# Folding mirrored rows on GpSimd, a ring of exp(k) rows, and the order of VectorE's taps in a two-block image kernel

## The chip, the cores and the metric

The kernel runs on one core of a Trainium2 chip, as one launch. The metric is device microseconds from the first to the last work of that launch, the median of several runs. One execution was also taken by the hardware profiler; all rows below are of that one.

## The reference

Eight images of 96 channels and 96 x 96 pixels go through two residual blocks, each behind a group norm of three channels a group (`x = x + L0(gn(x))`, `x = x + L1(gn(x))`), all in float32.

L0 makes four depthwise seven-tap filters of the image (along a row, a column and both diagonals), takes the mean of the squares of each, sends these 4 x 96 numbers through two small dense layers and a softmax over the four directions, adds up the four filtered images with these weights, and convolves the sum 3 x 3 with 96 x 96 channels.

L1 is attention over channels. It uses the image in two ways:

- `k = softmax(Wk x)` and `v = Wv x`, whose product over all pixels is a 24 x 24 context for each of four heads; `q = softmax(Wq x)`, times the context, times a projection, is `out`.
- `qf = real(ifft2(W_q2 gelu(W_q1 real(fft2(x)))))` and the keys from `out` give, normalized, a second channel attention, whose values are a 3 x 3 depthwise convolution of a projection of `out`.

The kernel before folds all small matrices of L1 into one 3 x 3 convolution of exp(q) per image. What needs the pixels is: the maxima of k and q, the two-dimensional Fourier transform of W_q1 x (with GELU behind it), exp(k) times v, the transform of exp(k), and Gram products of the two transforms.

## The kernel before, in words

Each of the five engines runs its own program: image 0's L0, then a loop in which the attention block (L1) of image b-1 runs beside the taps of L0 of image b, then the last L0, and the last L1 alone. Seven attention blocks so have another image's taps beside them, and the eighth has none. Engines wait for one another only by semaphores, in the order written. That order is by hand; no planner chooses it.

Within one attention block TensorE goes through a list of uses of five PSUM slots (`stage`, lines 901 to 910), and another engine empties each slot before its next use:

- 36 uses for the maxima of k and q (lines 950 to 957), which VectorE reduces (lines 708 to 712);
- 24 uses of four image rows each, W_q1 times x, written by ScalarE to `z` with the row index last (lines 526 to 530, 991 to 997);
- a first transform of 36 uses (`dft`, lines 959 to 974): for each 8 channels two uses of the first stage (four channels each, one product of 96 columns a channel against `w_dft`, cosines and sines side by side) and one use of the second stage (two products, with `dcos` and `dnsin`); ScalarE writes the first stage to `s1` and the second, through GELU, to `t_sp` (lines 532 to 540);
- 48 uses of two neighbouring rows each for k and v; ScalarE writes exp(k) to `z` and v to a ring of four (lines 542 to 546); three uses later TensorE adds v times exp(k) to the context (`ctx_rows`, lines 976 to 981), with exp(k) read from `z`, where neighbouring channels lie 96 elements apart;
- a second transform of 36 uses, of exp(k), and 49 Gram products (lines 1018 to 1024);
- 24 uses for exp(q), the e tiles (lines 983 to 987 and 548 to 556), mixed with a chain of small products for the attention weights.

Beside this VectorE and ScalarE make the next image's four filtered images in twelve units (`unit`, line 93): a unit is two directions of 16 rows. ScalarE makes the first tap of each direction and later squares the result (`unit_work`, lines 502 to 511); VectorE makes the other six taps of each, twelve instructions a unit (`taps`, lines 687 to 706). ScalarE puts its unit work between evictions, one piece every four uses, a new unit every `UNIT_USES` = 20 uses (lines 513 to 520). VectorE makes units 2 to 8 behind the maxima and only then begins the chain for the attention weights (`attention_weights`, line 728), which first waits for the Gram products; units 9 to 11 come behind it:

```
for u in range(2, LEAD):
    taps(b, u)
...
edge_rows(b, NCH - 1)
taps(b, LEAD, 0, LEAD_TAPS)
...
attention_weights(i, chain)
```

with `LEAD` = 8 and `LEAD_TAPS` = 12. ScalarE has its work for units 7 and 8 between the second transform and the e tiles (lines 608 to 612).

GpSimd clears padding, makes a few powers of single columns and issues the DMAs of the residual and the output; in the attention block its first instruction waits for the Gram products (line 399). SyncE issues the other DMAs, which the change leaves as they are.

Of the kernel before, what the change touches and what calls it, by code (L numbers as in the profile page):

```python
# [21 lines left out]
F32 = mybir.dt.float32  # L22
# [6 lines left out]
N = H * W  # L29
# [32 lines left out]

DFT_ORDER = []
for _j in range(C // 8 + 1):
    if _j < C // 8:
        DFT_ORDER += [(1, 2 * _j), (1, 2 * _j + 1)]
    if _j >= 1:
        DFT_ORDER.append((2, _j - 1))
assert len(DFT_ORDER) == U_DFT


# [55 lines left out]
def build(nc, a, out):  # L127
    with ExitStack() as ctx:
# [3 lines left out]
        def sem(name):  # L132
# [10 lines left out]
        z = nc.alloc_sbuf_tensor_at("z", [W, C, H], F32, offset=lo0)  # L143
        t_sp = nc.alloc_sbuf_tensor_at("t_sp", [H, NV, 2 * C], F32, offset=lo0 + H * C * 4)
        assert (H * C + NV * 2 * C) * 4 <= 2 * EBYTES
        SBYTES = CR * W * 4
        arena2 = sb("arena2", [128, SBYTES // 4])
        s0 = nc.sbuf_base - SBYTES

        s1 = nc.alloc_sbuf_tensor_at("s1", [H, 2, 8, W], F32, offset=s0)  # L150
        a32 = nc.alloc_sbuf_tensor_at("a32", [C, 9, C], F32, offset=s0)
# [6 lines left out]
        vrow = sb("vrow", [W, VROWS, 2, C])  # L158
        etile = sb("etile", [C, ETILES, TR * W])
        wp_hi, wp_lo = sb("wp_hi", [C, 9, C], F32R), sb("wp_lo", [C, 9, C], F32R)  # L160
        a_hi, a_lo = sb("a_hi", [C, 9, C], F32R), sb("a_lo", [C, 9, C], F32R)
        bk = sb("bk", [C, 9, C])
        wkv = sb("wkv", [C + 1, 2 * C])
        mats = sb("mats", [C, 12, C])
        ident, group, mask, negmask, w_dft, dcos, dnsin, wq, wq1, wq2, wq2t, wpft = (
            mats[:, i, :] for i in range(12))
        wc = sb("wc", [C, C])
# [61 lines left out]
        max_part = sem("max_part")  # L229
        stage_evac = sem("stage_evac")  # L230
        l1_small, l1_ps = sem("l1_small"), sem("l1_ps")
        maxrow_ready, gram_done, l1_pow, l1_exp = map(sem, ("maxrow_ready", "gram_done", "l1_pow", "l1_exp"))
# [16 lines left out]
        def rows(buf, r0, n, dx=0):  # L249

            at = (r0 + 1) * EP + 1 + dx
            return buf[:, at:at + n * EP].rearrange("p (r c) -> p r c", c=EP)[:, :, 0:W]

        def small_chain(eng, s, total, i):
# [54 lines left out]
        def _(sp):  # L309
            loads = [(mats[:, n, :], a[k]) for n, k in enumerate(  # L310
                ("ident", "group", "mask", "negmask", "w_dft", "dcos", "dnsin", "wq", "wq1", "wq2", "wq2t", "wpft"))]
            loads += [(wkv[0:C, :], a["wkv"]), (wh[:], a["wh"]), (wv[:], a["wv"]), (w45[:], a["w45"]),
# [66 lines left out]
        def _(pool):  # L379
# [5 lines left out]
            def zero_pads():  # L385
                for e in (e_hi, e_lo):
# [61 lines left out]
        def _(act):  # L448
# [83 lines left out]
            def dft(i, at, ch0, func):  # L532
                for n, (kind, g) in enumerate(DFT_ORDER):
                    ps = stage(i, at + n)
                    if kind == 1:
                        act.activation(s1[:, (g // 2) % 2, (g % 2) * 4:(g % 2) * 4 + 4, :],
                                       ps[0:H, 0:4 * W].rearrange("p (c v) -> p c v", v=W), ACT.Identity).then_inc(stage_evac, 1)
# [104 lines left out]
        def _(dve):  # L642
# [202 lines left out]
            def step(b, first, second, more):  # L845
# [9 lines left out]
                if first:  # L855
                    for u in range(2, LEAD):
                        taps(b, u)

                    dve.wait_ge(tap_done, unit_taps(b, LEAD - 1, KT - 1, 0 if first_image(b) else 1))
                    if first_image(b):  # L860
                        dve.wait_ge(last_dir_sums, LEAD)
# [32 lines left out]
        def _(pe):  # L894
# [64 lines left out]
            def dft(i, at):  # L959
                for n, (kind, g) in enumerate(DFT_ORDER):  # L960
                    ps = stage(i, at + n)
                    if kind == 1:
                        if g == 0:
                            evacuated(i, at - 1)
                        for c in range(4):
                            last = pe.matmul(ps[0:H, c * W:(c + 1) * W], z[:, 4 * g + c, :], w_dft, start=(c == 0), stop=(c == 3),  # L966
                                             skip_group_check=True)
                    else:
                        first_of = [k for k, v in enumerate(DFT_ORDER) if v == (1, 2 * g + 1)][0]
                        evacuated(i, at + first_of)  # L970
                        d = ps[0:H, 0:8 * NV].rearrange("p (c v) -> p c v", v=NV)
                        pe.matmul(d, dcos, s1[:, g % 2, :, 0:NV], start=True, stop=False)  # L972
                        last = pe.matmul(d[:, :, 1:NV - 1], dnsin, s1[:, g % 2, :, NV:W], start=False, stop=True)  # L973
                    last.then_inc(stage_full, 1)

            def ctx_rows(i, g):
                evacuated(i, AT_KV + g)
                for r in range(2):
                    last = pe.matmul(ctx_ps[0:C, 0:C], vrow[:, g % VROWS, r, :], z[:, :, 2 * g + r],  # L979
                                     start=(g == 0 and r == 0), stop=(g == U_KV - 1 and r == 1))  # L980
                return last
# [7 lines left out]
            def attention_block(i, between):  # L989
                maxes(i)  # L990
                for g in range(U_ROWS):
                    ps = stage(i, AT_ROWS + g)
                    for r in range(TR):
                        h = g * TR + r
                        last = pe.matmul(ps[0:W, r * C:(r + 1) * C], x1[0:C, h * W:(h + 1) * W], wq1,  # L995
                                         start=(r == 0), stop=(r == TR - 1), skip_group_check=True)
# [7 lines left out]
                for g in range(U_KV + BEHIND):  # L1004
                    if g < U_KV:
                        ps = stage(i, AT_KV + g)
                        for r in range(2):
                            h = 2 * g + r
                            last = pe.matmul(ps[0:W, r * 2 * C:(r + 1) * 2 * C], x1[:, h * W:(h + 1) * W], wkv[:],  # L1009
# [106 lines left out]

NAMES = ["x", "ident", "group", "mask", "negmask", "w_dft", "dcos", "dnsin", "wq", "wq1", "wq2", "wq2t", "wpft",
         "wkv", "wh", "wv", "w45", "w135", "wk3", "temp", "att1", "att2", "wp", "w_mid", "wkvv"]

# [49 lines left out]
```

## Time and profile before

| | before |
|---|---|
| median of 3 runs | 3964.45 us (3962.36 to 3966.53) |
| profiled execution | 3964.9 us, span 3963.1 us |
| TensorE busy | 3760.3 us, 95% |
| TensorE weight loads busy | 3091.5 us, 78% |
| VectorE busy | 3030.4 us, 76% |
| ScalarE busy | 1624.7 us, 41% |
| GpSimd busy | 210.3 us, 5% |
| granted TensorE clock, mean | 0.982 of 2.4 GHz |

Busy shares are means over the whole span: an engine at 76% can be at 100% in one stage and idle in another. In a timeline or a group of instructions a row gives start, duration, engine, line and shape; the bracket at the end is the idle time of the engine just before, and what ended it. Matmuls overlap, so their cost is read from start to start and not from the duration. A float32 product appears as two records. PE is TensorE's matmuls, PEld its weight loads, DVE VectorE, ACT ScalarE, POOL GpSimd.

### The profile page before, as it was taken

To read this page: it belongs to the slowest core of one execution; us is meant where nothing else is said; L and a number is where in the kernel's file an instruction comes from. 1 tells how busy PE (TensorE), PEld (TensorE's weight loads), DVE (VectorE), ACT (ScalarE), POOL (GpSimd) and SP (SyncE) were. 2 spreads that over 40 slices of the span, in tenths; PEclk is the share of its full clock that TensorE was granted. 3 is DMA by queue.
4 is the path that set the end of the run, shared out by engine and by line. 5 is a ranking of instruction groups with operands and counts; after the bars stand their busy time and mean duration, and the time that the engine had idled before them with its cause. 6 is when DMAs were issued, how large, how long until landed. Compare 5 with 4: busy or idle time off the path is not lost.

```text
span 3963.1 us, 56863 instructions
## 1 busy us (share of the span) xinstructions
PE 3760.3 (95%) x21394; PEld 3091.5 (78%) x21394; DVE 3030.4 (76%) x2829; ACT 1624.7 (41%) x2912; POOL 210.3 (5%) x376
## 2 busy tenths in 40 slices
PE   4659999999999999999999999999999999999998
PEld 2348788978799687977889787996879777897977
DVE  7988988789778898679887897789986797753020
ACT  3413662237521564126622375215641266202430
POOL 1001000100001000000001000010001000010000
PEclk8879999999999999999999999999999999999999
DMA  4354222923156221732228231562217322260002
GB/s 112 97 147 112 65 64 44 218 63 77 37 124 168 59 65 39 178 98 65 64 47 214 63 77 40 122 166 60 68 36 194 82 74 55 53 163 25 1 7 30
DMA packets 164717, 344.13 MB, mean 87 GB/s; under 512 B 110336, under 2 KB 110576, under 8 KB 164432
## 3 DMA queue, kind: packets, MB, share of 16 engines
q1 hardware_dynamic: 141392, 255.36, 26.1%
q0 software_dynamic: 23040, 84.95, 9.8%
q8 instruction: 181, 2.97, 0.3%
q14 instruction: 104, 0.85, 0.1%
HBM read 189.27 MB, written 150.99 MB: 86 GB/s over the span
## 4 chain that ended last, share of the span: by engine, by line
PE 77%; DVE 12%; issue 7%; ACT 2%; DMA 1%; POOL 0%; SPq 0%; DVEq 0%; ACTq 0%; POOLq 0%
PE banks L941 15%; PE banks L942 15%; PE banks L947 15%; DVE feat L702 7%; PE banks L979 6%; PE banks L956 6%; PE banks L1009 6%; PE banks L966 4%; PE banks L1021 3%; PE banks L972 2%; PE banks L973 2%; DVE e_lo L725 2%; DMA feat<-feats_d 1%; DVE e_hi L718 1%; PE banks L995 0%
## 5 line engine op out<-in xcount | busy, mean ns | idle before, releaser
L702 DVE SCALAR_TENSOR_TENSOR feat<-xin,w,feat 96x1536 f32<-96x1536 f32 x540 | 943.2, 1808 | 1.1
L941 PE MATMUL banks<-e_hi,wp_hi 96*96 96x384 f32 x1728 | 587.6, 341 | 23.4 <-DVE e_lo L828 12.0
L941 PE MATMUL banks<-e_hi,a_hi 96*96 96x384 f32 x1728 | 591.9, 343 | 15.2 <-ACT a_hi L572 15.2
L942 PE MATMUL banks<-e_lo,a_hi 96*96 96x384 f32 x1728 | 590.1, 342 | 0.0
L942 PE MATMUL banks<-e_lo,wp_hi 96*96 96x384 f32 x1728 | 586.6, 340 | 0.0
L702 DVE SCALAR_TENSOR_TENSOR feat<-xin,wh,feat 96x1536 f32<-96x1536 f32 x288 | 520.5, 1807 | 43.8 <-ACT feat L488 42.9
L702 DVE SCALAR_TENSOR_TENSOR feat<-xin,wv,feat 96x1536 f32<-96x1536 f32 x288 | 520.5, 1807 | 8.9 <-ACT feat L488 8.9
L500 ACT ACTIVATE sqjunk<-feat 96x1536 bf16<-96x1536 f32 x192 | 284.4, 1481 | 258.7 <-DVE feat L702 255.8
L563 ACT ACTIVATE res<-banks 96x768 f32<-96x768 f32 x96 | 77.5, 808 | 689.2 <-PE banks L947 689.2
L947 PE MATMUL banks<-e_hi,a_lo 96*96 96x384 f32 (+1 forms) x1728 | 337.1, 339 | 0.0
L947 PE MATMUL banks<-e_hi,wp_lo 96*96 96x384 f32 (+1 forms) x1728 | 336.1, 338 | 0.0
L966 PEld LDWEIGHTS banks<-mats,z 96*96 96x96 f32 x3072 | 288.0, 165 | 57.7 <-issue 46.8
L941 PEld LDWEIGHTS banks<-e_hi,wp_hi 96*96 96x96 f32 x1728 | 281.3, 163 | 51.4 <-DVE e_lo L828 12.4
L941 PEld LDWEIGHTS banks<-e_hi,a_hi 96*96 96x96 f32 x1728 | 283.3, 164 | 48.6 <-issue 16.1
L979 PE MATMUL banks<-z,vrow 96*96 96x96 f32 x1536 | 312.9, 339 | 3.5 <-ACT vrow L546 3.5
L1009 PE MATMUL banks<-wkv,x 97*96 97x192 f32 x1536 | 315.5, 328 | 0.0
L942 PEld LDWEIGHTS banks<-e_lo,a_hi 96*96 96x96 f32 x1728 | 283.8, 164 | 27.7
L942 PEld LDWEIGHTS banks<-e_lo,wp_hi 96*96 96x96 f32 x1728 | 281.6, 163 | 27.6
L947 PEld LDWEIGHTS banks<-e_hi,a_lo 96*96 96x96 f32 x1728 | 279.6, 163 | 26.4
L947 PEld LDWEIGHTS banks<-e_hi,wp_lo 96*96 96x96 f32 x1728 | 278.6, 162 | 26.1
L966 PE MATMUL banks<-mats,z 96*96 96x96 f32 x3072 | 289.9, 248 | 2.6 <-ACT z L529 2.6
L1009 PEld LDWEIGHTS banks<-wkv,x 97*96 97x96 f32 x1536 | 255.8, 170 | 7.1 <-issue 6.3
(147 smaller groups left out, 4921.7 us busy)
## 6 DMA issues: line engine op xcount, KB each, us to landing
feats_d<-feat SPq DMA_DIRECT2D x160, 576.0 KB, 4.1
feat<-feats_d SPq DMA_DIRECT2D x160, 576.0 KB, 6.5
feat<-in_x SPq DMA_DIRECT2D x48, 576.0 KB, 7.1
res<-in_x POOLq DMA_DIRECT2D x96, 288.0 KB, 4.1
out<-x POOLq DMA_DIRECT2D x96, 288.0 KB, 2.8
out<-res POOLq DMA_DIRECT2D x96, 288.0 KB, 4.4
xin<-in_x SPq DMA_DIRECT2D x32, 792.0 KB, 8.9
xin<-in_x SPq DMA_DIRECT2D x16, 684.0 KB, 9.9
```

The source lines that it names most:

```text
L500: act.activation(sqjunk[:], feat[:, d], ACT.Square, accum_out=sq[:, d, ch:ch + 1]).then_inc(squared, 1)
L702: dve.scalar_tensor_tensor(out=dst, in0=src, scalar=taps_w[d](k), in1=dst, op0=ALU.mult, op1=ALU.add).then_inc(tap_done, 1)
L725: dve.tensor_tensor(rows(e_lo, t * TR, TR), etile[:, t % ETILES].rearrange("p (r c) -> p r c", c=W), rows(e_hi, t * TR, TR).bitcast(F32), ...
L941: pe.matmul(dst, whi[:, t, :], rows(e_hi, a0, n, dx), start=(t == CENTRE_FIRST[0]), stop=False)
L942: pe.matmul(dst, whi[:, t, :], rows(e_lo, a0, n, dx), start=False, stop=False)
L947: last = pe.matmul(dst, wlo[:, t, :], rows(e_hi, a0, n, dx), start=False, stop=(t == CENTRE_LAST[-1]))
L956: pe.matmul(ps[0:C, :], w, x1[0:C, t * BANK:(t + 1) * BANK], start=True, stop=True)\
L966: last = pe.matmul(ps[0:H, c * W:(c + 1) * W], z[:, 4 * g + c, :], w_dft, start=(c == 0), stop=(c == 3), skip_group_check=True)
L972: pe.matmul(d, dcos, s1[:, g % 2, :, 0:NV], start=True, stop=False)
L979: last = pe.matmul(ctx_ps[0:C, 0:C], vrow[:, g % VROWS, r, :], z[:, :, 2 * g + r], start=(g == 0 and r == 0), stop=(g == U_KV - 1 and r == 1))
L1009: last = pe.matmul(ps[0:W, r * 2 * C:(r + 1) * 2 * C], x1[:, h * W:(h + 1) * W], wkv[:], start=(r == 0), stop=(r == 1), skip_group_check=True)
L1021: pe.matmul(gram_ps[0:C, 2 * C:4 * C], t_sp[:, v, 0:C], t_sp[:, v, :], start=(v == 1), stop=(v == NV - 2))
```

## The change

Rows h and 96-h enter a Fourier transform along h with the same cosine and opposite sines. The change adds and subtracts such rows before the transform, in both uses.

- GpSimd writes `xf`, the sums (49 rows) and differences (47 rows) of normalized image rows, in `fold_x`; W_q1 is applied to those. It waits chunk by chunk for the normalized image, and TensorE waits for all of it before its 24 uses.
- The k,v uses take rows g and 96-g instead of two neighbours. ScalarE writes exp(k) not to `z` but to a ring of six row pairs (`krow`, in the memory of the e tiles). The context product reads that ring. GpSimd reads it too, and writes sums and differences to `z` (`fold_k`: 49 instructions an image). ScalarE waits for `k_folded` before it writes over a pair, and TensorE waits for all folds before the second transform.
- The transform has 24 uses instead of 36. A use of the first stage takes 8 channels, each with two products of 49 columns: 49 summed rows (in a block of 64) with cosines to partitions 0 to 63, 47 differences with sines to partitions 64 to 110. The second stage is one product over those 111 partitions with `dh`. The order is 8 first, 4 second, 4 first, 8 second. `s1` has eight slots, in two pieces of memory.
- `UNIT_USES` is 18. VectorE's loop is rewritten around `last_use` = 7; `LEAD_TAPS` is gone.

The diff, cut:

```
-U_DFT = C // 4 + C // 8
+U_DFT = 2 * (C // 8)
...
+DFT_ORDER = ([(1, g) for g in range(8)] + [(2, g) for g in range(4)]
+             + [(1, g) for g in range(8, 12)] + [(2, g) for g in range(4, 12)])
+KROWS = 6
+X_FOLDS = [(41, 7)] + [(h, 8) for h in range(33, 0, -8)]
...
-LEAD_TAPS = TAPS // 2
-UNIT_USES, UNIT_AT = 20, AT_ROWS + 8
+UNIT_USES, UNIT_AT = 18, AT_ROWS + 8
...
+            def fold_x(i):
+                v = x1[0:C, :].rearrange("p (h x) -> p h x", x=W)
+                for h, n in X_FOLDS:
+                    up, down = v[:, h:h + n, :], v[:, H - h:H - h - n:-1, :]
+                    pool.wait_ge(xn_ready, i * XN + -(-(H - h + 1) * W // (N // XN)))
+                    pool.tensor_tensor(xf[:, h:h + n, :], up, down, ALU.add).then_inc(x_folded, 1)
+                    pool.tensor_tensor(xf[:, NV - 1 + h:NV - 1 + h + n, :], up, down, ALU.subtract).then_inc(x_folded, 1)
+                pool.tensor_copy(xf[:, 0:NV:NV - 1, :], v[:, 0:NV:NV - 1, :]).then_inc(x_folded, 1)
+            def fold_k(i):
...
+                def fold(g, n):
+                    s = g % KROWS
+                    one_, other = krow[:, s:s + n, 0, :], krow[:, s:s + n, 1, :]
+                    pool.tensor_tensor(z[:, :, g:g + n].rearrange("p c h -> p h c"), one_, other, ALU.add)\
+                        .then_inc(k_folded, 1)
+                    at = NV - 1 + g
+                    pool.tensor_tensor(z[:, :, at:at + n].rearrange("p c h -> p h c"), one_, other, ALU.subtract)\
+                        .then_inc(k_folded, 1)
+                row_evicted(1)
+                fold(1, 1)
+                pool.tensor_copy(z[:, :, 0:NV:NV - 1].rearrange("p c h -> p h c"), krow[:, 0, :, :]).then_inc(k_folded, 1)
+                for g in range(2, U_KV, 2):
+                    row_evicted(g + 1)
+                    fold(g, 2)
...
+                    fold_x(i)
+                    fold_k(i)
                     pool.wait_ge(gram_done, i + 1)
...
-                    act.activation(z[:, :, 2 * g:2 * g + 2], ps[:, :, 0:C].rearrange("p r c -> p c r"), ACT.Exp)
+                    if g >= KROWS:
+                        act.wait_ge(k_folded, i * K_FOLD_OPS + k_folds((g - KROWS) // 2 + 1))
+                    act.activation(krow[:, g % KROWS], ps[:, :, 0:C], ACT.Exp)
...
-                    for u in range(2, LEAD):
+                    last_use = UNITS - 5
+                    for u in range(2, last_use + 1):
                         taps(b, u)
...
-                    taps(b, LEAD, 0, LEAD_TAPS)
+                    for u in range(last_use + 1, LEAD + 1):
+                        taps(b, u)
                 if second:
                     attention_weights(i, chain)
                 if first:
-                    taps(b, LEAD, LEAD_TAPS)
...
-                        for c in range(4):
-                            last = pe.matmul(ps[0:H, c * W:(c + 1) * W], z[:, 4 * g + c, :], w_dft, start=(c == 0), stop=(c == 3),
-                                             skip_group_check=True)
+                        for c in range(8):
+                            cols = slice(c * NV, (c + 1) * NV)
+                            pe.matmul(ps[0:ODD_AT, cols], z[:, 8 * g + c, 0:ODD_AT], w_cos[:, 0:NV], start=(c == 0),
+                                      stop=(c == 7), skip_group_check=True)
+                            last = pe.matmul(ps[ODD_AT:FOLDED, cols], z[:, 8 * g + c, NV:W], w_sin[:, 0:NV],
+                                             start=(c == 0), stop=(c == 7), skip_group_check=True)
...
-                        pe.matmul(d, dcos, s1[:, g % 2, :, 0:NV], start=True, stop=False)
-                        last = pe.matmul(d[:, :, 1:NV - 1], dnsin, s1[:, g % 2, :, NV:W], start=False, stop=True)
+                        last = pe.matmul(ps[0:H, 0:8 * NV], dh[:], s1(g).rearrange("p c v -> p (c v)"), start=True, stop=True)
...
+                pe.wait_ge(x_folded, (i + 1) * X_FOLD_OPS)
...
+                pe.wait_ge(k_folded, (i + 1) * K_FOLD_OPS)
                 dft(i, AT_DFT2)
```

## Rows read from the trace of the kernel before

**Rows 1.** The page, part 4, the chain of waits, by engine.
```profile
PE 77%; DVE 12%; issue 7%; ACT 2%; DMA 1%; POOL 0%; SPq 0%; DVEq 0%; ACTq 0%; POOLq 0%
```

**Rows 2.** Busy time by stretch of one steady image; columns in the first line.
```profile
core 0: us, PE busy (x) PEld busy (x) DVE busy (x) ACT busy (x) POOL busy (x), PEclk, DMA share, GB/s
845.40:876.40 31.00, 30.97 (x72) 11.82 (x73) 28.80 (x39) 11.00 (x16) 0.00 (x0) 1.00 0.17 45
876.40:894.50 18.10, 17.74 (x198) 16.67 (x196) 17.76 (x13) 15.85 (x31) 0.00 (x0) 1.00 0.20 37
894.50:927.90 33.40, 32.39 (x240) 24.18 (x241) 33.40 (x21) 28.14 (x49) 0.00 (x0) 1.00 0.39 96
927.90:992.40 64.50, 64.00 (x387) 63.10 (x386) 64.50 (x38) 43.24 (x114) 0.00 (x0) 1.00 0.26 69
...
1068.00:1305.40 237.40, 235.80 (x1328) 211.65 (x1327) 186.03 (x165) 48.93 (x48) 23.11 (x38) 1.00 0.54 127
```

**Rows 3.** Timeline of VectorE in that image; start us, us, instruction, idle before.
```profile
877.65 1.81 DVE L702 SCALAR_TENSOR_TENSOR feat<-xin,wh,feat 96x1536 f32<-96x1536 f32 x1
879.38 1.80 DVE L702 SCALAR_TENSOR_TENSOR feat<-xin,wv,feat 96x1536 f32<-96x1536 f32 x1
...
1025.28 1.81 DVE L702 SCALAR_TENSOR_TENSOR feat<-xin,wv,feat 96x1536 f32<-96x1536 f32 x1
1041.48 0.25 DVE L732 TENSOR_TENSOR ctxm<-banks,mats 96x96 f32<-96x96 f32 x1 [14.39 <-PE banks L1023]
```

**Rows 4.** Timeline of ScalarE before the e tiles of that image.
```profile
1032.47 1.48 ACT L500 ACTIVATE sqjunk<-feat 96x1536 bf16<-96x1536 f32 x1
...
1033.96 1.92 ACT L468 ACTIVATE xin<-xin,xpar 96x1824 f32<-96x1824 f32 x1
...
1037.60 1.58 ACT L488 ACTIVATE feat<-xin,wv 96x1536 f32<-96x1536 f32 x1
1042.57 0.58 ACT L555 ACTIVATE etile<-banks,nmax 96x384 f32<-96x384 f32 x1 [3.39 <-POOL e_lo L390]
```

**Rows 5.** Timeline of TensorE in the k,v stage and in the second transform.
```profile
964.20 0.83 PE L1009 MATMUL banks<-wkv,x 97*96 97x192 f32 x4
964.86 0.82 PE L979 MATMUL banks<-z,vrow 96*96 96x96 f32 x4
965.51 0.83 PE L1009 MATMUL banks<-wkv,x 97*96 97x192 f32 x4
...
995.18 0.83 PE L972 MATMUL banks<-s,mats 96*96 96x392 f32 x2
995.84 0.79 PE L973 MATMUL banks<-s,mats 96*96 96x376 f32 x2
996.47 1.52 PE L966 MATMUL banks<-mats,z 96*96 96x96 f32 x16
997.83 0.83 PE L972 MATMUL banks<-s,mats 96*96 96x392 f32 x2
```

**Rows 6.** The chain in the last image's attention block; start us, us, what.
```profile
3645.53 16.32 PE banks L995 x192
...
3667.09 1.36 PE banks L966 x16
3669.74 1.36 PE banks L966 x16
```

**Rows 7.** Timeline of TensorE's weight loads with few moving columns.
```profile
1139.62 0.43 PEld L1083 LDWEIGHTS banks<-l0v,att 96*48 96x48 f32 x8 [0.28 <-issue]
1145.03 0.75 PEld L1090 LDWEIGHTS banks<-hid,att 48*96 48x96 f32 x8 [0.28 <-issue]
```

**Rows 8.** Timeline of GpSimd.
```profile
0.99 3.83 POOL L435 MEMSET xin<- 96x4488 f32 x1 [0.29 <-POOLq L1160]
...
842.48 0.56 POOL L383 TENSOR_TENSOR gpar<-gpar,consts 96x1 f32<-96x1 f32 x1 [2.20 <-DVE gpar L674]
1041.61 0.17 POOL L388 MEMSET e_hi<- 96x97 f32 x1 [198.57 <-PE banks L1023]
1041.73 0.17 POOL L389 MEMSET e_hi<- 96x99 f32 x1
```

**Rows 9.** Timeline of ScalarE, normalizing the image between the blocks.
```profile
843.60 12.80 ACT L587 ACTIVATE x<-x,x1par 96x512 f32<-96x512 f32 x18 [22.82 <-DVE x1par L678]
```

**Rows 10.** VectorE's groups from 960 to 1050 us: busy, mean ns, idle before.
```profile
L702 DVE SCALAR_TENSOR_TENSOR feat<-xin,wv,feat 96x1536 f32<-96x1536 f32 x12 | 21.8, 1813 | 1.3 <-ACT feat L488 1.3
L702 DVE SCALAR_TENSOR_TENSOR feat<-xin,wh,feat 96x1536 f32<-96x1536 f32 x12 | 21.7, 1812 | 2.2 <-ACT feat L488 2.2
```

More of the change, by code:

```diff
@@ L60, with k_folds @@
 USES = AT_E + U_E
[L63 to L68, printed above, removed]
-assert len(DFT_ORDER) == U_DFT
+DFT_ORDER = ([(1, g) for g in range(8)] + [(2, g) for g in range(4)]
+             + [(1, g) for g in range(8, 12)] + [(2, g) for g in range(4, 12)])
+assert len(DFT_ORDER) == U_DFT
+NO = W - NV
+ODD_AT = 64
+FOLDED = ODD_AT + NO
+S1 = 8
+KROWS = 6
+X_FOLDS = [(41, 7)] + [(h, 8) for h in range(33, 0, -8)]
+X_FOLD_OPS = 2 * len(X_FOLDS) + 1
+def k_folds(n):
+    return 2 * n + 1 if n else 0
+K_FOLD_OPS = k_folds(H // 4)
 CENTRE_FIRST = (4, 0, 1, 2, 3, 5, 6, 7, 8)
@@ L159, in build @@
         etile = sb("etile", [C, ETILES, TR * W])
+        krow = etile[0:W].rearrange("p t n -> p (t n)").rearrange("p (s r c) -> p s r c", s=KROWS, r=2)
         wp_hi, wp_lo = sb("wp_hi", [C, 9, C], F32R), sb("wp_lo", [C, 9, C], F32R)
-        a_hi, a_lo = sb("a_hi", [C, 9, C], F32R), sb("a_lo", [C, 9, C], F32R)
-        bk = sb("bk", [C, 9, C])
+        ABYTES = 9 * C * 4
+        arena3 = sb("arena3", [128, 3 * ABYTES // 4])
+        k0 = nc.sbuf_base - 3 * ABYTES
+        a_hi = nc.alloc_sbuf_tensor_at("a_hi", [C, 9, C], F32R, offset=k0)
+        a_lo = nc.alloc_sbuf_tensor_at("a_lo", [C, 9, C], F32R, offset=k0 + ABYTES)
+        bk = nc.alloc_sbuf_tensor_at("bk", [C, 9, C], F32, offset=k0 + 2 * ABYTES)
+        s1b = nc.alloc_sbuf_tensor_at("s1b", [FOLDED, S1 - 3, 8, NV], F32, offset=k0)
+        assert (S1 - 3) * 8 * NV * 4 <= 3 * ABYTES
         wkv = sb("wkv", [C + 1, 2 * C])
-        mats = sb("mats", [C, 12, C])
-        ident, group, mask, negmask, w_dft, dcos, dnsin, wq, wq1, wq2, wq2t, wpft = (
-            mats[:, i, :] for i in range(12))
+        mats = sb("mats", [C, 11, C])
+        ident, group, mask, negmask, w_cos, w_sin, wq, wq1, wq2, wq2t, wpft = (mats[:, i, :] for i in range(11))
+        dh = sb("dh", [FOLDED, H])
         wc = sb("wc", [C, C])
@@ L310, in _ @@
             loads = [(mats[:, n, :], a[k]) for n, k in enumerate(
-                ("ident", "group", "mask", "negmask", "w_dft", "dcos", "dnsin", "wq", "wq1", "wq2", "wq2t", "wpft"))]
+                ("ident", "group", "mask", "negmask", "w_cos", "w_sin", "wq", "wq1", "wq2", "wq2t", "wpft"))]
+            loads += [(dh[:], a["dh"])]
             loads += [(wkv[0:C, :], a["wkv"]), (wh[:], a["wh"]), (wv[:], a["wv"]), (w45[:], a["w45"]),
@@ L962, in dft @@
                     if kind == 1:
-                        if g == 0:
+                        if g == 0 and at == AT_DFT1:
                             evacuated(i, at - 1)
-                        for c in range(4):
-                            last = pe.matmul(ps[0:H, c * W:(c + 1) * W], z[:, 4 * g + c, :], w_dft, start=(c == 0), stop=(c == 3),
-                                             skip_group_check=True)
-                    else:
-                        first_of = [k for k, v in enumerate(DFT_ORDER) if v == (1, 2 * g + 1)][0]
-                        evacuated(i, at + first_of)
-                        d = ps[0:H, 0:8 * NV].rearrange("p (c v) -> p c v", v=NV)
-                        pe.matmul(d, dcos, s1[:, g % 2, :, 0:NV], start=True, stop=False)
-                        last = pe.matmul(d[:, :, 1:NV - 1], dnsin, s1[:, g % 2, :, NV:W], start=False, stop=True)
+                        for c in range(8):
[4 more added lines that the diff above has]
+                                             start=(c == 0), stop=(c == 7), skip_group_check=True)
+                    else:
+                        evacuated(i, at + DFT_ORDER.index((1, g)))
+                        last = pe.matmul(ps[0:H, 0:8 * NV], dh[:], s1(g).rearrange("p c v -> p (c v)"), start=True, stop=True)
                     last.then_inc(stage_full, 1)
@@ L978, in ctx_rows @@
                 for r in range(2):
-                    last = pe.matmul(ctx_ps[0:C, 0:C], vrow[:, g % VROWS, r, :], z[:, :, 2 * g + r],
+                    last = pe.matmul(ctx_ps[0:C, 0:C], vrow[:, g % VROWS, r, :], krow[:, g % KROWS, r, :],
                                      start=(g == 0 and r == 0), stop=(g == U_KV - 1 and r == 1))
@@ L993, in attention_block @@
                     for r in range(TR):
-                        h = g * TR + r
-                        last = pe.matmul(ps[0:W, r * C:(r + 1) * C], x1[0:C, h * W:(h + 1) * W], wq1,
+                        last = pe.matmul(ps[0:W, r * C:(r + 1) * C], xf[:, g * TR + r, :], wq1,
                                          start=(r == 0), stop=(r == TR - 1), skip_group_check=True)
@@ L1114, in _ @@
             steps(pe, start, step)
-NAMES = ["x", "ident", "group", "mask", "negmask", "w_dft", "dcos", "dnsin", "wq", "wq1", "wq2", "wq2t", "wpft",
-         "wkv", "wh", "wv", "w45", "w135", "wk3", "temp", "att1", "att2", "wp", "w_mid", "wkvv"]
+NAMES = ["x", "ident", "group", "mask", "negmask", "w_cos", "w_sin", "wq", "wq1", "wq2", "wq2t", "wpft",
+         "dh", "wkv", "wh", "wv", "w45", "w135", "wk3", "temp", "att1", "att2", "wp", "w_mid", "wkvv"]
 def kernel(x, L0_conv_w_h, L0_conv_w_v, L0_conv_w_d45, L0_conv_w_d135, L0_conv_w_att1, L0_conv_w_att2,
@@ L1142 @@
         "negmask": np.where(same, 0.0, -1e30).astype(f),
-        "w_dft": np.concatenate([cos[:, :NV], sin[:, 1:NV - 1]], 1).astype(f),
-        "dcos": cos.astype(f),
-        "dnsin": (-sin).astype(f),
+        "w_cos": np.where(n < NV, cos, 0.0).astype(f),
+        "w_sin": np.where((n > 0) & (n < NV - 1), sin, 0.0).astype(f),
+        "dh": np.concatenate([cos[:NV], np.zeros((ODD_AT - NV, W)), -sin[1:NV - 1]]).astype(f),
         "wq": qkv[0:C].T, "wkv": qkv[C:3 * C].T,
```

19 lines of the change are left out of this document (13 added, 6 removed).

## The prediction, made before the changed kernel was run

> **What bounds the kernel now.** I read the page's chain first: 77% of it is TensorE and 12% VectorE [rows 1], so on average TensorE sets the time. The change touches one stretch of each image's attention half, so I then read one steady image stage by stage [rows 2]; from its first product of the maxima (845.4 us) to that of the next image it is 460.0 us. The edits lie between 876.4 and 1041.5. TensorE is busy there nearly without a gap, at a granted clock of 1.00 (the 2.4 GHz level), but VectorE is at 98 to 100% too from 876.4 to 992.4. This second fact decides the case. VectorE makes 84 taps one behind the other, from 877.65 to 1027.1, and then stands idle for 14.39 us until TensorE's last Gram product lets its attention chain begin [rows 3]. ScalarE squares unit 8, normalizes the last chunk, makes unit 10's first taps, is through at 1039.2, and makes its first e tile at 1042.57 [rows 4]. So TensorE may come earlier by some 14 us, and no more, before VectorE is what is waited for.
>
> **The change part by part.**
>
> *Context from the ring.* Each row pair costs four records of the k,v product and four of the context product, 0.66 and 0.65 us [rows 5]. The context product streams 96 elements that lie 96 apart in z: 163 ns a record. L995 streams 96 that lie together, and 192 records take 16.32 us, 85 ns each [rows 6]. A row of the ring lies together, so I take 85. 192 records an image times 78 ns: 15.0 us gained, 64.5 to 49.5 for the stage.
>
> *Half transforms.* A group of 8 channels now costs 2.65 us (995.18 to 997.83): the second-stage products 0.66 and 0.63, and 16 first-stage records 1.36 [rows 5]. After it, the second stage is one product of 392 columns, 0.66. The first stage has 32 records of 49 moving columns with 64 or 47 weight columns. At 85 ns per 96 columns, 49 stream in 44 ns. What a weight load allows shows in two small groups: with 48 weight columns and one moving column 8 loads pass in 0.43 us, with 96 in 0.75 [rows 7]; less the last one's own 0.13 and 0.16, over seven steps, that is 43 and 84 ns each. So 56 ns for 64 columns, 44 for 47; a channel costs 2 x 56 + 2 x 44 = 200 ns, a group 1.60, with the second stage 2.26. 0.39 x 12 = 4.7 us a transform, 9.4 an image. The bounds: both column halves side by side, 8 x 2 x 56 = 0.90 (13 us gained a transform); every record at L966's 85 ns, 2.72 (8.8 lost). I take the weight-load value, whose rows are nearest in size.
>
> *fold_x.* GpSimd has nothing to do from 843.0 to 1041.6 [rows 8], and what is queued there behind the folds (pads, the power, the output DMAs) waits for the Gram products anyway. The folds are 12 instructions with 9024 results and a copy of 192. GpSimd's cheapest element is a memset's, 3.83 us for 4488, 0.85 ns; small memsets start 0.12 us apart [rows 8]. Two operands at 0.85 each and 13 starts make 17 us. It begins when the eleventh of eighteen normalized chunks is there, 843.60 + 11 x 0.71 = 851.4 [rows 9], and ends near 869, under TensorE's maxima, which last to 876.4. That cover holds to 25 us, 2.7 ns a result; beyond it TensorE waits. Four taps of VectorE fall into this stretch; held up by folds, they delay the end of the maxima by perhaps 2 us.
>
> *fold_k.* 49 instructions, most with 192 results. At the same prices one takes 384 x 0.85 + 120 = 0.45 us, 0.9 for two row pairs, which TensorE brings in 2 us: GpSimd keeps up if it runs undisturbed. ScalarE waits for the ring, six row pairs back, and TensorE for the last folds, 1.5 us. ScalarE is busy 43 of 64.5 us in this stage [rows 2], evicts 24 tiles fewer in the two transforms, and stays under TensorE.
>
> *What the folds do to VectorE.* A tap reads two tensors in SBUF while a fold reads two as well, and no row of this trace shows both at it together. The ends: no effect; or each excludes the other, so that a fold waits for the tap in front of it (1.73 us from start to start [rows 3]) and the next tap for the fold. Between them VectorE stands still while a fold reads: 0.33 us for its reads, 0.45 for the whole instruction. I take 0.40, 49 x 0.40 = 19.6 us an image, with 2 more from fold_x; it is the value nearest to the memset rows, and both ends stay in the range.
>
> *VectorE's order.* LEAD_TAPS was 12, all of unit 8, so units 2 to 8 came before the chain and still do; the edited loops issue the same taps in the same order. That phrase of the change is worth nothing. ScalarE's unit work, spaced 18 uses for 20, follows the shorter stage list: unit 8's first taps come some 9 us earlier, and the 2.2 and 1.3 us that VectorE waited for them [rows 10] go.
>
> **Sum for a middle image.** TensorE alone: 15.0 + 9.4 - 1.5, 23 us, of which ScalarE's waits for VectorE's taps take perhaps 5; Gram products end near 1023. VectorE: 1027.1 - 3.5 + 21.6 = 1045.2. ScalarE then needs the second square, the norm and two first taps, 6.8 us (1032.47 to 1039.18 [rows 4]): e tiles begin at 1052.0 instead of 1042.57, 9.4 later. What was TensorE's gain is idle time. Later stages shift by as much. Seven images have taps beside their attention half, 7 x 9.4 = 66; the eighth has none, its groups repeat every 2.65 us without VectorE [rows 6], and TensorE keeps its 23. 66 - 23 = +43 us. The profiled execution took 3964.9 (span 3963.1), the median is 3964.45, so nothing is to be corrected: 4007.
>
> **The rivals.**
>
> *No contention.* Nothing in the profile speaks against it but the want of a row. VectorE ends at 1023.6, e tiles begin at 1030.4, 12.2 earlier; 7 x 12.2 + 23 = 108 us: 3856. VectorE is then the bound, so a dearer or cheaper transform changes little. Only at 2.72 for the first stage does TensorE bound again: it gains 15.0 and loses 17.6 + 1.5, 4.1 us an image, 8 x 4.1 = 33: 3997.
>
> *Folds and taps exclude each other.* Taps start 1.73 us apart and each lasts 1.81 [rows 3], without a gap. A fold that waits for one then costs 1.73 + 0.45 = 2.18 us, 49 of them 107 us, in a stage that needs 49.5. The ring of six makes ScalarE and so TensorE wait: k,v rows end at 1029, the transform's eighteenth use, with unit 8's first taps, comes at 1054, these taps end at 1073, e tiles begin at 1080, 37 later. 7 x 37 - 23 = +239: 4203. If GpSimd gets in only where VectorE lacks first taps, about 4225. The Trainium skill speaks for this rival: the page "SBUF — State Buffer", section "Who interferes with whom", says that a VectorE instruction with two SBUF inputs contends with a GpSimd instruction that reads SBUF, and that whichever started first holds the shared ports for the whole instruction. No row here shows it; by that rule the time is 4203, by free access 3856.
>
> My forecast is slower from 15.5 us of lost VectorE time an image on (12.2 + 23 / 7), 0.28 us a fold beside the 2 of fold_x.
>
> **How the numbers follow.** Forecast 0.38 (3983 to 4075 by 0.33 to 0.60 us a fold); no contention 0.32; exclusion 0.25; dear transforms without contention 0.05. About 0.2% (8 us) is what a measurement of this kernel can tell from no change. Faster: 0.32, and 0.05 of the forecast, with folds under 0.26 us; within 0.2%: 0.06; slower: the rest of the forecast, 0.27, with 0.25 and 0.05, is 0.57. The range goes from past the no-contention time to the exclusion time, 3845 to 4205; the likeliest case alone has 3983 to 4075.
>
> **What would show it.** Right: the context product at 85 ns a record, groups at 2.26 us, L732 no longer waiting for L1023, taps 2.1 us apart where folds run and 1.73 elsewhere, a k,v stage near 50 us. Taps at 1.73 throughout and e tiles near 1030 would mean no contention. Folds over 1 us each, ScalarE waiting for the ring before its Exp and a k,v stage near 100 us would mean exclusion. A wait of TensorE before its U rows would mean that fold_x takes over 25 us. If taps are stretched and the kernel is still faster, the forecast's main step, that VectorE takes over the bound, is wrong.

## The result, and the profile after

The changed kernel takes 4224.4 us (median of 4 runs, 4223.5 to 4227.1) against 3965.5 (4 runs) for the kernel before: ratio 1.0655, 95% interval 1.0637 to 1.0674. The forecast was 4007, the range 3845 to 4205: the direction is right, the time is outside. The rival *folds and taps exclude each other* had 4203, and its tail, "if GpSimd gets in only where VectorE lacks first taps", 4225.

The chain of waits by engine, in the changed kernel's page [rows 1]:

```profile
PE 52%; issue 20%; POOL 13%; DVE 11%; DMA 2%; ACT 2%; SPq 0%; DVEq 0%; POOLq 0%; ACTq 0%
```

TensorE's share falls from 77 to 52%. GpSimd, absent before, holds 13%, and 20% is time in which an engine waited for nothing that the profile shows. The same steady image stage by stage [rows 2] (us, then busy time of each engine, the mean granted clock, DMA):

```profile
891.30:938.97 47.67, 33.03 (x72) 12.34 (x73) 44.58 (x39) 11.00 (x16) 22.77 (x13) 0.86 0.12 30
938.97:957.00 18.03, 17.71 (x197) 16.64 (x195) 17.69 (x13) 15.77 (x30) 0.00 (x0) 1.00 0.20 36
957.00:981.00 24.00, 20.73 (x412) 15.69 (x412) 24.00 (x15) 18.58 (x30) 0.00 (x0) 1.00 0.19 55
981.00:1078.00 97.00, 59.91 (x402) 54.33 (x404) 86.00 (x45) 44.74 (x120) 88.36 (x49) 0.78 0.26 65
1078.00:1105.00 27.00, 26.42 (x395) 20.96 (x392) 12.26 (x9) 18.37 (x32) 0.00 (x0) 0.71 0.30 72
1105.00:1121.40 16.40, 16.40 (x101) 16.13 (x102) 16.40 (x10) 7.39 (x8) 0.00 (x0) 1.00 0.06 16
1121.40:1155.00 33.60, 27.12 (x72) 12.16 (x72) 24.77 (x69) 23.55 (x56) 1.47 (x7) 0.85 0.09 29
1155.00:1394.00 239.00, 237.35 (x1329) 213.05 (x1328) 185.84 (x165) 49.08 (x49) 23.25 (x38) 0.99 0.54 126
```

The image grows from 460.0 to 502.7 us, 42.7: maxima +16.7, U rows -0.1, first transform -9.4, k,v stage +32.5, second transform with the Gram products -5.7 (43.4, before 49.1), chain and e tiles to the first convolution +7.1 (33.6, before 26.5), convolutions +1.6. Seven images make 7 x 42.7 = 299 us. The last one, without taps, is 39.1 shorter: 192.1 us from its first maximum to the attention chain before, 153.0 after. 299 - 39 = 260; the medians differ by 259. (The bound between the first transform and the k,v stage is put at 981.0 here. TensorE makes its first k,v product at 977.05 and then waits 4.25 us for ScalarE to empty PSUM slots; with the bound at that product, where it lies before, the transform takes 20 us and the k,v stage 101.) So there are two losses, both in stages where GpSimd works: 47.67 instead of 31.0, and 97.0 instead of 64.5.

The first, VectorE, GpSimd and TensorE in the maxima stage (start, duration, instruction):

```profile
898.23 2.48 DVE L761 SCALAR_TENSOR_TENSOR feat<-xin,w,feat 96x1536 f32<-96x1536 f32 x1
900.63 4.26 DVE L770 TENSOR_REDUCE mx<-banks 96x1 f32<-96x512 f32 x7
904.82 17.00 DVE L761 SCALAR_TENSOR_TENSOR feat<-xin,w,feat 96x1536 f32<-96x1536 f32 x1
```

```profile
903.96 1.86 POOL L425 TENSOR_TENSOR xf<-x 96x768 f32<-96x768 f32 x1
905.74 1.88 POOL L424 TENSOR_TENSOR xf<-x 96x768 f32<-96x768 f32 x1
...
918.08 1.85 POOL L425 TENSOR_TENSOR xf<-x 96x768 f32<-96x768 f32 x1
919.82 0.39 POOL L426 COPY xf<-x 96x192 f32<-96x192 f32 x1
```

```profile
922.48 2.02 PE L1016 MATMUL banks<-x,mats 96*96 96x512 f32 x2 [14.60 <-DVE mx L770]
```

The tap that starts at 904.82 lasts 17.00 us instead of 1.81: it ends at 921.82, 1.6 us after the last fold, so nine folds, back to back, and the copy behind them went first. Behind it stand the maxima, and TensorE waits 14.60 us for a free PSUM slot.

In the k,v stage it is the other way round, GpSimd, then VectorE, then ScalarE, which waits for the ring:

```profile
987.05 17.49 POOL L436 TENSOR_TENSOR z<-etile 96x96 f32<-96x96 f32 x1 [66.84 <-ACT vrow L605]
1004.49 0.39 POOL L439 TENSOR_TENSOR z<-etile 96x96 f32<-96x96 f32 x1
...
1006.85 0.60 POOL L439 TENSOR_TENSOR z<-etile 96x192 f32<-96x192 f32 x1
1007.39 0.60 POOL L436 TENSOR_TENSOR z<-etile 96x192 f32<-96x192 f32 x1
1007.95 2.15 POOL L439 TENSOR_TENSOR z<-etile 96x192 f32<-96x192 f32 x1
1010.06 2.11 POOL L436 TENSOR_TENSOR z<-etile 96x192 f32<-96x192 f32 x1
```

```profile
986.90 1.81 DVE L761 SCALAR_TENSOR_TENSOR feat<-xin,wv,feat 96x1536 f32<-96x1536 f32 x1
988.64 1.81 DVE L761 SCALAR_TENSOR_TENSOR feat<-xin,wh,feat 96x1536 f32<-96x1536 f32 x1
...
1002.47 1.81 DVE L761 SCALAR_TENSOR_TENSOR feat<-xin,w,feat 96x1536 f32<-96x1536 f32 x1
1007.83 22.49 DVE L761 SCALAR_TENSOR_TENSOR feat<-xin,w,feat 96x1536 f32<-96x1536 f32 x11 [3.55 <-ACT feat L545]
1041.37 2.15 DVE L761 SCALAR_TENSOR_TENSOR feat<-xin,wh,feat 96x1536 f32<-96x1536 f32 x1
1043.44 2.14 DVE L761 SCALAR_TENSOR_TENSOR feat<-xin,wv,feat 96x1536 f32<-96x1536 f32 x1
```

```profile
1005.35 0.33 ACT L604 ACTIVATE etile<-banks 96x192 f32<-96x192 f32 x1 [14.63 <-POOL z L443]
```

The first fold stands for 17.49 us while taps run undisturbed, 1.73 apart as before [rows 3], and gets in at 1004.3, when VectorE lacks a first tap. Without taps folds pass every 0.55 us. When taps come again, each fold takes turns with one tap, both 2.07 us apart. The ring of six stands full, ScalarE stops (14.63 us the first time) and with it TensorE (59.91 us busy of 97), and the mean granted clock falls to 0.78 and, in the second transform, 0.71. First taps, issued by ScalarE between stage uses, come late in turn. VectorE ends its taps at 1121.4:

```profile
1121.43 0.25 DVE L791 TENSOR_TENSOR ctxm<-banks,mats 96x96 f32<-96x96 f32 x1
1128.91 0.36 DVE L777 CAST e_hi<-etile 96x384 fp32r<-96x384 f32 x1 [6.46 <-ACT etile L614]
```

No wait for the Gram products stands before the chain any more (14.39 us in [rows 3]): VectorE is now the one waited for, as forecast, but far later.

### The profile page after: what moved, and what is told of

It reads as the page before. It is cut to its first block, busy times and chain, and to the rows that moved or that the text cites. A ratio compares the mean times of both kernels' runs of the same rounds, so it can differ in the third digit from the quotient of the medians.

```text
span 4225.5 us, 62917 instructions
## 1 busy us (share of the span) xinstructions
PE 3653.6 (86%) x24082; PEld 2966.3 (70%) x24082; DVE 3215.7 (76%) x2829; ACT 1525.5 (36%) x2720; POOL 1040.9 (25%) x872
## 4 chain that ended last, share of the span: by engine, by line
PE 52%; issue 20%; POOL 13%; DVE 11%; DMA 2%; ACT 2%; SPq 0%; DVEq 0%; POOLq 0%; ACTq 0%
PE banks L1001 14%; PE banks L1002 14%; PE banks L1007 14%; DVE feat L761 7%; POOL z L439 5%; POOL z L436 5%; PE banks L1027 3%; POOL xf L425 1%; PE banks L1016 1%; PE banks L1033 1%; DVE e_lo L784 1%; POOL xf L424 1%; PE banks L1046 1%; PE banks L1069 1%; DMA feats_d<-feat 1%
## 5 line engine op out<-in xcount | busy, mean ns | idle before, releaser
L761 DVE SCALAR_TENSOR_TENSOR feat<-xin,w,feat 96x1536 f32<-96x1536 f32 x540 | 1100.4, 2097 | 25.9 <-ACT feat L545 24.9
L761 DVE SCALAR_TENSOR_TENSOR feat<-xin,wh,feat 96x1536 f32<-96x1536 f32 x288 | 532.6, 1849 | 152.0 <-ACT feat L545 151.2
L761 DVE SCALAR_TENSOR_TENSOR feat<-xin,wv,feat 96x1536 f32<-96x1536 f32 x288 | 532.5, 1849 | 35.2 <-ACT feat L545 35.2
L436 POOL TENSOR_TENSOR z<-etile 96x192 f32<-96x192 f32 (+1 forms) x192 | 377.2, 1965 | 547.6 <-ACT vrow L605 547.6
L1069 PE MATMUL banks<-wkv,x 97*96 97x192 f32 x1536 | 375.7, 376 | 29.6 <-ACT t_sp L596 29.6
L1039 PE MATMUL banks<-etile,vrow 96*96 96x96 f32 x1536 | 228.9, 281 | 150.4 <-ACT vrow L605 150.4
L1039 PEld LDWEIGHTS banks<-etile,vrow 96*96 96x96 f32 x1536 | 217.1, 192 | 176.5 <-ACT vrow L605 172.1
L468 POOL DMA_DIRECT2D out<-res x96 | 77.3, 806 | 1044.7 <-ACT res L622 1035.6
L1069 PEld LDWEIGHTS banks<-wkv,x 97*96 97x96 f32 x1536 | 265.8, 194 | 50.3 <-ACT t_sp L596 32.8
```

Of the source, the lines that this page charges most:

```text
L436: pool.tensor_tensor(z[:, :, g:g + n].rearrange("p c h -> p h c"), one_, other, ALU.add)\
L761: dve.scalar_tensor_tensor(out=dst, in0=src, scalar=taps_w[d](k), in1=dst, op0=ALU.mult, op1=ALU.add).then_inc(tap_done, 1)
```

## The experiments

One measure serves for all: from VectorE's first maximum to its first e tile in the second attention image, 196.6 us before, 236.4 after (the rest of the image takes 264 to 268 us everywhere).

| kernel | time, us | ratio to before, 95% | maximum to e tile, us |
|---|---|---|---|
| changed | 4224.4 | 1.0637 to 1.0674 | 236.4 |
| exp(k) folds as memsets | 3956.3 | 0.9955 to 0.9988 | 202.5 |
| exp(k) folds as copies | 4135.8 | 1.0378 to 1.0451 | 228.4 |
| taps behind the maxima | 4144.3 | 1.0429 to 1.0464 | 226.3 |
| memsets, taps behind the maxima | 3890.7 | 0.9785 to 0.9818 | 191.1 |
| three row pairs a fold, taps behind | 4079.3 | 1.0263 to 1.0298 | 218.7 |
| memset between taps, taps behind | 4129.9 | 1.0389 to 1.0424 | 227.9 |
| both of these, taps behind | 4034.2 | 1.0165 to 1.0196 | 212.0 |
| all folds as memsets | 3839.7 | 0.9666 to 0.9701 | 184.1 |
| only x folded, taps behind | 3947.5 | 0.9933 to 0.9967 | 196.7 |
| the same, shorter way to the e tiles | 3914.3 | 0.9852 to 0.9885 | 190.1 |
| the same, last image fully folded | 3888.3 | 0.9798 to 0.9825 | 190.3 |

**Is it the folds' reads?** The folds of exp(k) as memsets, then as copies of one operand:

```diff
-pool.tensor_tensor(z[:, :, g:g + n].rearrange("p c h -> p h c"), one_, other, ALU.add)
+pool.memset(z[:, :, g:g + n].rearrange("p c h -> p h c"), 1.0)       # first run
+pool.tensor_copy(z[:, :, g:g + n].rearrange("p c h -> p h c"), one_)  # second run
```

> GpSimd's 49 instructions of the folding of exp(k) become memsets of the same outputs (the folding of exp(k) is left out; GpSimd writes as much, waits for the same rows and signals the same semaphores, but reads nothing). Theory, VectorE's taps and GpSimd's reading instructions keep each other out of the SBUF ports: the taps of the k,v stage come 1.73 us apart again (1.8 to 2.1 and stand-stills of 17 us in the changed kernel), no memset waits behind the taps, the k,v stage falls from 97 us to 48 to 64 us, TensorE's clock stays up through the second transform (27.0 us to about 22), the tap of 17 us in the maxima stage stays, and the time falls by 7 x 40 to 50 us, from 4224 to 3870 to 3945 us. Rival A, the ring of six rows and its round of semaphores, or GpSimd's own rate for strided outputs, is too slow: the k,v stage stays at 90 us or more and the time within 1% of 4224. Rival B, it is the write traffic of the ports: the same as A.

> The same 48 sums and differences as copies of one of their two operands (the folding of exp(k) is left out; GpSimd reads half as much and writes as much). Theory, any GpSimd instruction that reads SBUF is kept out whole, and keeps the taps out: the k,v stage keeps stand-stills of 10 us and more and stays at 85 to 100 us, the time at 4150 to 4230 us. Rival C, the ports share by bytes, and each side slows in proportion to what the other reads: the loss of the k,v stage is about halved, 72 to 82 us, and the time 4060 to 4130 us. Rival D, only GpSimd instructions with two SBUF inputs are kept out: the k,v stage falls to 48 to 64 us and the time to 3870 to 3945 us.

Memsets give 268 us back: semaphores, ring and writes are innocent. The time, 3956, is 11 us above the expected bounds; the k,v stage (61 us) and the second transform (22 us) are as expected. A memset is also shorter than a sum (0.43 to 0.53 us against 0.59), but GpSimd's own rate is not what is too slow: in the changed kernel's last image, where no tap runs, sums pass every 0.55 us and its 153.0 us differ little from the 152.6 with memsets. Copies give 89 back, and no theory had that whole: 4136 lies between rival C's bounds and the theory's. Their trace settles it, GpSimd and then VectorE:

```profile
973.58 17.35 POOL L437 COPY z<-etile 96x96 f32<-96x96 f32 x1 [68.36 <-ACT vrow L606]
...
1024.48 1.98 POOL L437 COPY z<-etile 96x192 f32<-96x192 f32 x1
1026.32 1.96 POOL L440 COPY z<-etile 96x192 f32<-96x192 f32 x1
```

```profile
1024.16 1.90 DVE L762 SCALAR_TENSOR_TENSOR feat<-xin,wv,feat 96x1536 f32<-96x1536 f32 x1
1025.99 1.90 DVE L762 SCALAR_TENSOR_TENSOR feat<-xin,wh,feat 96x1536 f32<-96x1536 f32 x1
```

Copies are shut out and take turns just as sums do; a turn is 1.83 us instead of 2.07, since a copy keeps the tap away for 0.10 us and a sum for 0.34. Their k,v stage is 86 us (90 from the first k,v product), inside the theory's bounds and above rival C's. Rival D falls, and C with it: not a share by bytes, but turns.

**The stand-still in the maxima stage.**

```diff
-for n in range(MAX_TAPS + 1):
-    maxes(i, n * U_MAX // (MAX_TAPS + 1), (n + 1) * U_MAX // (MAX_TAPS + 1))
-    if first and n < MAX_TAPS:
-        taps(b, 1, EARLY_TAPS + n, EARLY_TAPS + n + 1)
+maxes(i, 0, U_MAX)
...
+if first:
+    taps(b, 1, EARLY_TAPS, TAPS // 2)
```

> The four taps that stand between the maxima are made right behind them, so no tap runs beside the folding of x (nothing is left out). Theory: no tap of 17 us, the maxima stage falls from 47.7 us to 28 to 32 us, the folding of x takes its 21.5 us as in the last image, the four taps cost 7 us that VectorE has to spare there, and the k,v stage stays as it is: about 12 to 18 us an image less, 4100 to 4140 us. Rival, the maxima stage is slow because GpSimd's folding of x itself takes the ports of TensorE's or ScalarE's reads: the stage stays above 40 us and the time at 4210 to 4230 us.

> Both edits: memsets for the folding of exp(k) (left out), and the four taps behind the maxima. Theory: the sum of the two, since each takes another stand-still away: 3770 to 3860 us, with the taps 1.73 us apart everywhere but for the memsets, and an image at 440 us or less (502.7 in the changed kernel, 460.0 in the kernel before). Rival, the stand-stills share one cover (VectorE's slack ahead of the attention chain): no more than the better of the two alone, 3870 us or more.

The first gives 80 us; its maxima stage is back at 31 us, its maximum to e tile is 10 us shorter than the changed kernel's, and its time, 4144, is 4 above the bounds. The second came out at 3891, 31 above its bounds: its rival is not right either, since 3891 is 66 below the better of the two edits alone (3956). The four taps placed behind the maxima cost VectorE 7 us that it did not have to spare there, as the next run shows.

**The rival of no contention itself.** All folds as memsets, the taps where the change has them:

```diff
-pool.tensor_tensor(xf[:, h:h + n, :], up, down, ALU.add).then_inc(x_folded, 1)
+pool.memset(xf[:, h:h + n, :], 0.5).then_inc(x_folded, 1)
```

> The changed kernel with all of GpSimd's folds, of x and of exp(k), as memsets of the same outputs (both foldings are left out; order, waits and signals stay, the four taps stand between the maxima as in the changed kernel). This is the rival of no contention of the prediction in itself. That rival's sum: 3856 us, the e tiles 12 us earlier than in the kernel before (196.6 us from the first maximum to the first e tile, so about 184). Theory, all of the changed kernel's loss is the folds' reads: 3830 to 3870 us, below the 3891 us of the run with both edits, whose taps behind the maxima cost VectorE 7 us an image there. Rival, the memsets' writes or the four taps hold the maxima up as well: 3885 us or more.

3839.7 us: that rival's 3856 was 16 too high. Its stages, maxima to Gram products:

```profile
835.50:866.30 30.80, 30.80 (x75) 11.80 (x74) 28.76 (x40) 10.97 (x16) 8.24 (x13) 1.00 0.19 48
866.30:884.40 18.10, 17.74 (x205) 16.67 (x205) 17.93 (x12) 16.03 (x31) 0.00 (x0) 1.00 0.18 33
884.40:908.40 24.00, 20.48 (x410) 15.43 (x405) 24.00 (x15) 18.66 (x29) 0.00 (x0) 0.99 0.20 58
908.40:966.10 57.70, 52.86 (x382) 50.26 (x382) 57.70 (x35) 44.55 (x120) 18.97 (x49) 0.92 0.37 88
966.10:986.40 20.30, 19.77 (x408) 15.10 (x408) 20.30 (x12) 17.76 (x31) 0.00 (x0) 1.00 0.20 61
```

With the reads gone the maxima are back at 30.8, the k,v stage at 57.7 (62 from the first k,v product; ScalarE, before it squares units, waits for VectorE 9.6 us between 884 and 966) and the second transform at 20.3, at full clock. The loss adds up: 4224 - 3956 = 268 us for exp(k)'s reads, 3956 - 3840 = 117 for x's, 385 in all, if they are taken away in this order.

**Why does the first fold wait 17 us and the later ones one tap?** On the kernel with taps behind the maxima:

```diff
 dve.scalar_tensor_tensor(out=dst, in0=src, ..., in1=dst, ...).then_inc(tap_done, 1)
+if gaps:                                   # units 4 to 7
+    dve.memset(gap[:, n:n + 1], 0.0)
```

> On the kernel with the four taps behind the maxima (4144 us): a memset of one element a partition follows each tap of units 4 to 7 on VectorE (about 0.06 us each; nothing is left out). It asks why the first fold of each image waits 17 us while later ones wait for one tap each. Theory E, the fold isn't let in because the next tap follows the one before without a gap: with the memsets between, the first fold of every image starts within one tap (under 2.5 us in place of 17.5), the ring doesn't stand full there, and the time falls by up to 7 x 8 us or stays, since folds still take turns at 2.1 us or more with taps: 4090 to 4160 us. Theory F, the ports stay with VectorE as long as a tap is ready, whatever stands between: the first fold still lasts about 17.5 us and the time stays at 4140 to 4170 us.

```profile
958.49 1.96 POOL L437 TENSOR_TENSOR z<-etile 96x96 f32<-96x96 f32 x1 [58.14 <-ACT vrow L606]
960.41 1.90 POOL L440 TENSOR_TENSOR z<-etile 96x96 f32<-96x96 f32 x1
```

A memset of 0.06 us between taps lets the fold in at the next tap's end: 1.96 us instead of 17.48 in the run it builds on. Theory E holds. The time hardly moves (4130 against 4144), because 49 folds at one tap each still take 90 us.

**Fewer, larger folds.**

```diff
-row_evicted(1)
-fold(1, 1)
+row_evicted(2)
+fold(1, 2)
...
-for g in range(2, U_KV, 2):
-    row_evicted(g + 1)
-    fold(g, 2)
+for g in range(3, U_KV, 3):
+    row_evicted(g + 2)
+    fold(g, 3)
```

> On the kernel with the four taps behind the maxima (4144 us): exp(k) folded three row pairs at a time in place of two, 33 instructions an image in place of 49 with the same elements in all (nothing is left out). Theory, folds and taps take turns, one whole instruction each, so that a fold costs its turn and hardly its size: with turns of 2.1 to 2.3 us the k,v stage falls from about 97 us to 72 to 85 us, and the time by 12 to 22 us an image, to 3990 to 4060 us. Rival, the ports are shared by bytes or GpSimd is bound by its elements: the stage and the time stay within 1% of 4144 us.

> Both at once: folds of three row pairs (33 instructions an image) and the memset between taps (nothing is left out). Theory of turns: each fold instruction waits for one tap and no first one for ten, so the k,v stage is 33 turns of 2.27 us, 75 us, some of them without a tap: 66 to 76 us against 81 with three row pairs alone; time 4030 to 4070 us against 4079 and 4130 us for either alone. Rival, the memsets only shift the stand-still to another place: 4079 us or more.

With three row pairs a turn is 2.27 us (1.73 for the tap, 0.54 for the fold) and there are 33 of them. From the first fold's start to the last one's end it is 81 us, against 90 in the run it builds on; the time, 4079, misses the expected 4060 by 19. With the memsets as well it is 74 us and 4034, inside. The cost of a fold is one tap and a little of its size. These versions stay slower than the kernel before.

**Towards a version that keeps the gain.** Only x folded, where VectorE reads PSUM; then ten taps ahead of the maxima, and ScalarE's unit 8 behind the e tiles; then the last image, without taps, folded in full:

```diff
-            for u in range(LEAD - 1 if second else 1, LEAD + 1):
+            for u in range(LEAD - 1 if second else 1, LEAD if second else LEAD + 1):
...
             a_split(i)
+            if first:
+                unit_work(b, LEAD)
...
+if last_image(i):
+    fold_k(i)
```

> Only x is folded: the first transform runs on half as many columns, while exp(k), its context product and the second transform are done as in the kernel before (nothing is left out), and the four taps stand behind the maxima, so that GpSimd's folds never meet a tap. Theory: taps 1.73 us apart throughout, the maxima stage 31 us, the first transform 24 us instead of 33; TensorE's Gram products end about 12 us earlier, but VectorE's taps end some 4 us later than before, so an image gains 3 to 5 us and the last image 12: 3915 to 3935 us. Rival, the half transform gains nothing beside the taps: 3960 to 3970 us.

> As the run with only x folded, with two things taken off VectorE's path to the e tiles: ten instead of eight taps of the second unit are made ahead of the maxima and two behind them, and ScalarE makes the squares, the norm and the first taps of its last unit behind the e tiles instead of ahead of them (6.8 us there; nothing is left out). Theory, in the run with only x folded VectorE and these ScalarE steps set when the e tiles begin: 5 to 8 us an image less, 3865 to 3895 us. Rival, TensorE sets it: within 0.3% of the run with only x folded.

> The run with only x folded and the shorter way to the e tiles (3914 us), and in the last image, which has no taps beside it, exp(k) folded by GpSimd from the ring as well, with the context from the ring and the second transform on half as many columns (nothing is left out). Theory, the folds cost nothing where no tap runs: the last image's attention half is shorter by the other 26 of the 39 us that the changed kernel gained there, 3885 to 3893 us, and the seven images before it stay as they are. Rival, the ring or GpSimd's rate binds in the last image too: 3905 us or more.

The first two miss, 13 and 19 us above their bounds. The last image gains its 12 us (192.1 to 180.0), but beside taps the Gram products come only 2 us earlier (192.8 us behind the first maximum, 194.9 before). The first transform is 10 us shorter there, and the k,v stage 7 us longer (71.7 for 64.5, at a mean granted clock of 0.93): ScalarE squares a unit at a fixed use of TensorE's, which now comes before VectorE has finished the unit (13.7 us of such waits from the U rows to the Gram products, 1.9 before), and TensorE stands idle 5.2 us behind it. ScalarE's waits of the kind in the whole run (total, times, longest), with only x folded:

```profile
ACT sqjunk L546 <- DVE feat L758: 331.3, 87, 20.9
```

Before they were 255.8 us, 66 times. The two edits of the second run give 33 us together; which gives how much was not taken apart. The third does what was expected: its last image takes 153.0 us, as in the changed kernel, with folds undisturbed:

```profile
3653.31 0.59 POOL L457 TENSOR_TENSOR z<-etile 96x192 f32<-96x192 f32 x1
3653.86 0.59 POOL L460 TENSOR_TENSOR z<-etile 96x192 f32<-96x192 f32 x1
```

3888.3 us, 1.9% below the kernel before (interval 1.8 to 2.0%), with nothing left out: it beats both kernels. It also has the two edits of the second run, which are no part of the folding; what they would give the kernel before by themselves, no run shows.

## Why the prediction was wrong

- **The step that failed**: "VectorE stands still while a fold reads ... I take 0.40", beside "GpSimd keeps up". It took one number from between the two ends, but the ends were two mechanisms. What it says of VectorE was nearly right: a fold costs a tap 0.34 us. What it left out is the other side, that a fold waits for a whole tap: 2.07 us a fold, where TensorE needs 0.99 us a row pair. The rival had priced that at 2.18, and the sentence on it (taps "without a gap") held the reason why a fold does not get in at all at first. The Trainium skill, page "SBUF — State Buffer", section "Who interferes with whom", was cited for that rival. On who excludes whom the traces agree: taps with two SBUF inputs and GpSimd's reads exclude each other, memsets, which only write, run beside taps at 0.43 to 0.53 us with the taps 1.73 us apart, and reductions from PSUM keep 0.69 us beside folds. Where the Trainium skill's page has the first one hold the ports for its whole instruction, the traces have less: a fold of 0.59 us keeps a tap back for 0.34. And a fold that had come first was not let in first: nine taps that started later went ahead of the one that had stood since 987.05.
- **The chance.** Exclusion had 0.25, with a page of the Trainium skill for it and no row against it; 0.40 us a fold had 0.38, with neither such a page nor a row for it. The rival's 4203 was low mostly because it had no stand-still in the maxima stage: "perhaps 2 us" were 16.7 an image, 117 us in all. It was too high elsewhere, since folds pass in 0.55 us while VectorE lacks taps, and its last image gained 23 us instead of 39. That its tail's 4225 lies within 1 us of the result is therefore luck: folds were shut out until VectorE lacked a first tap only at the first fold of an image, and took turns with taps after that.
- **fold_x**: 17 us forecast, 21.5 measured where no tap runs (last image, 3924.5 to 3946.0), inside the cover of 25. A fold of 192 results: 0.45 forecast, 0.55 measured. That gap was small; the rate was never the trouble.
- **Context product**: 85 ns forecast and measured, 0.34 us for four records. **Transforms**: 2.26 us a group forecast, 1.59 measured: first stages come 0.93 us apart and second ones 0.66, near the lower bound (0.90), which had both column halves side by side. So the last image gained 39 us (15.0 + 2 x 12.7 - 1.5), not 23. The chain in the last image, then ScalarE's evictions:

```profile
3988.61 0.65 PE banks L1069 x4
3989.27 0.34 PE banks L1039 x4
3989.61 0.65 PE banks L1069 x4
```

```profile
3968.20 0.50 ACT L593 ACTIVATE s1a<-banks 111x392 f32<-111x392 f32 x1 [0.44 <-PE banks L1029]
3969.14 0.50 ACT L593 ACTIVATE s1a<-banks 111x392 f32<-111x392 f32 x1 [0.44 <-PE banks L1029]
...
3984.58 0.49 ACT L596 ACTIVATE t_sp<-banks 96x392 f32<-96x392 f32 x1 [0.17 <-PE banks L1033]
3985.23 0.49 ACT L596 ACTIVATE t_sp<-banks 96x392 f32<-96x392 f32 x1 [0.17 <-PE banks L1033]
```

- **VectorE's order** issues the same taps in the same order, as said; no run varied it, or `UNIT_USES`, alone. **The clock** was not in the sum: with TensorE idle in the k,v stage, the second transform ran at a mean of 0.71 and took 27.0 us instead of 20.3.
- Left open: why a tap waits behind nine back-to-back folds of x and their copy (17.00 us) in most images, while in one image of the run with copies taps and folds of x took turns. No run varied GpSimd's succession.

## What to carry to other kernels

When two engines may exclude each other, price both sides: what the fast one loses, and how long the slow one waits, which is the other's instruction length times the number of instructions. Put the work of the slow engine where the other reads PSUM or is idle, and if it can't be moved, make it few and large. A cost bounded by two mechanisms is not their mean.

## What the runs showed of the hardware

- Back-to-back taps (1.73 us apart) kept a fold out for 17 us; one VectorE memset of 0.06 us between taps let it in at the next tap's end (its duration fell from 17.48 to 1.96 us).
- VectorE loses less than GpSimd's instruction lasts (a turn less the tap's 1.73 us): a copy of 0.52 us takes 0.10 us from a tap, a sum of 0.59 takes 0.34, one of 0.80 takes 0.54.
